# Three buffers for the halves of x, an earlier split of R, and the tile sets of each block built in one go, in a four-block modulated residual convolution

## The reference

```python
for k in range(4):                       # blocks L0 .. L3, each with its own weights
    out = x
    for i, typ in enumerate(('same', 'upsample', 'same', 'downsample')):
        out = _layer(out, cond_512, weights[i], biases[i], mod_w[i], mod_b[i], typ)
    x = x + out

def _layer(x, style, w, b, mw, mb, typ):
    s = style @ mw.T + mb                                  # a scale per sample and input channel
    weight = SCALE * w * s[:, None, :, None]
    demod = lax.rsqrt(jnp.sum(weight * weight, axis=(2, 3)) + EPS)
    weight = weight * demod[:, :, None, None]              # one 64 x 64 x 3 filter per sample
    if typ == 'same':         out = conv(x, weight, pad 1) + b
    elif typ == 'upsample':   out = blur(conv_transpose(x, weight, stride 2) + b, 2 * blur_k, (1, 1))
    elif typ == 'downsample': out = conv(blur(x, blur_k, (2, 2)), weight, stride 2) + b
```

## Time and profile before

| What | Value |
|---|---|
| median of 3 runs | 1443.01 us |
| the profiled execution's own time | 1441.61 us |
| its span, first to last instruction | 1439.8 us |
| busy: PE, PEld | 1405.6 us (98%), 1184.3 us (82%) |
| busy: DVE, ACT, POOL | 1017.6 us (71%), 701.8 us (49%), 380.8 us (26%) |
| granted TensorE clock | 1.00 (the 2.4 GHz level) in every slice |
| DMA queues, together | 39.65 MB, 28 GB/s |

### The profile page before, as it was taken

One profiled execution on the slowest core, in us unless ns is written; L12 is line 12 of the kernel. 1 busy time (PEld: TensorE's weight loads), 2 busy tenths in 40 slices (PEclk: granted clock), 3 DMA queues, 4 the chain that ended last, 5 costly groups with the idle time before them and its releaser, 6 DMA issues.

```text
span 1439.8 us, 21306 instructions
## 1 busy us (share of the span) xinstructions
PE 1405.6 (98%) x7436; PEld 1184.3 (82%) x7436; DVE 1017.6 (71%) x1634; ACT 701.8 (49%) x1132; POOL 380.8 (26%) x778
## 2 busy tenths in 40 slices
PE   5999999989999999999999999999999999999998
PEld 4777878878888888888888888888888888888886
DVE  8887978876676676677576676676676676676674
ACT  5445444536545445445555445445555444444454
POOL 4533332252322121221321222121231311212121
PEclk9999999999999999999999999999999999999999
DMA  6000000001530000000241000000042000000004
GB/s 225 7 1 1 7 1 2 5 1 65 140 95 1 1 1 1 0 1 1 64 114 59 1 1 0 1 1 1 1 110 67 0 1 1 1 1 1 1 16 102
DMA packets 20632, 39.65 MB, mean 28 GB/s; under 512 B 1840, under 2 KB 3248, under 8 KB 20528
## 3 DMA queue, kind: packets, MB, share of 16 engines
q1 hardware_dynamic: 20096, 37.87, 9.2%
q10 hardware_dynamic: 432, 0.43, 0.1%
HBM read 21.48 MB, written 16.81 MB: 27 GB/s over the span
## 4 chain that ended last, share of the span: by engine, by line
PE 90%; DVE 6%; ACT 1%; issue 1%; DMA 0%; POOL 0%; ACTq 0%; POOLq 0%; DVEq 0%
PE ps L361 28%; PE ps L363 27%; PE ps L362 27%; PE ps L368 3%; PE ps L367 3%; PE ps L458 1%; PE ps L477 1%; DVE gl L811 1%; DVE xl L763 1%; PE ps L468 1%; DVE vl L795 1%; DVE vh L794 1%; DVE gl L815 0%; PE ps L448 0%; ACT vh L595 0%
## 5 line engine op out<-in xcount | busy, mean ns | idle before, releaser
L575 ACT ACTIVATE zh<-ps,t_bx 128x512 fp32r<-128x512 f32 x256 | 176.3, 689 | 680.6 <-PE ps L363 676.8
L361 PE MATMUL ps<-zh,gh 128*128 128x512 f32 x1024 | 411.5, 402 | 0.2 <-DVE gl L815 0.2
L363 PE MATMUL ps<-zh,gl 128*128 128x512 f32 x1024 | 404.4, 395 | 0.0
L362 PE MATMUL ps<-zl,gh 128*128 128x512 f32 x1024 | 404.3, 395 | 0.0
L769 DVE SCALAR_TENSOR_TENSOR zl<-ps,t_bx,zh 128x512 fp32r<-128x512 f32 x256 | 190.6, 745 | 93.3 <-ACT zh L575 91.7
L363 PEld LDWEIGHTS ps<-zh,gl 128*128 128x128 f32 x1024 | 194.2, 190 | 46.1
L362 PEld LDWEIGHTS ps<-zl,gh 128*128 128x128 f32 x1024 | 193.9, 189 | 41.3
L779 DVE SCALAR_TENSOR_TENSOR X<-ps,t_D,X 128x511 f32<-128x511 f32 x256 | 190.7, 745 | 51.6 <-PE ps L363 51.4
L361 PEld LDWEIGHTS ps<-zh,gh 128*128 128x128 f32 x1024 | 193.0, 189 | 41.4 <-issue 0.3
L361 PE MATMUL ps<-xh,w0h 128*128 128x512 f32 x512 | 206.6, 403 | 8.1 <-DVE xl L763 8.1
L363 PE MATMUL ps<-xh,w0l 128*128 128x512 f32 x512 | 203.3, 397 | 0.0
(11 more groups left out here) (143 smaller groups left out, 2017.7 us busy)
## 6 DMA issues: line engine op xcount, KB each, us to landing
X<-x_in SPq DMA_DIRECT2D x32, 513.0 KB, 6.4
out_x<-X SPq DMA_DIRECT2D x64, 256.5 KB, 4.0
pk<-taps_in SPq DMA_DIRECT2D x3, 512.0 KB, 11.9
pk<-pack_in SPq DMA_DIRECT2D x3, 352.0 KB, 11.1
pk<-sets_in SPq DMA_DIRECT2D x4, 192.0 KB, 2.4
pk<-taps_in SPq DMA_DIRECT2D x2, 144.0 KB, 4.6
pk<-pack_in ACTq DMA_DIRECT2D x1, 224.0 KB, 3.1
w3f<-w_in SPq DMA_DIRECT2D x1, 192.0 KB, 10.5
```

Of the source, the lines that this page charges most:

```text
L361: pe.matmul(out_ap, ah, bh, start=first, stop=False, skip_group_check=True)
L362: pe.matmul(out_ap, ah, bl, start=False, stop=False, skip_group_check=True)
L363: return pe.matmul(out_ap, al, bh, start=False, stop=last, skip_group_check=True)
L575: act.activation(zh[n % 2][:, ZPAD:ZPAD + M], ps[:, ZP + n % 2, :], IDENT, bias=tab["bx"][:, k, b:b + 1]).then_inc(s["zhi"], 1)
```

## The change

Three parts. (1) `xh` and `xl` have three buffers each, and `xhi` and `xlo` run for sample n+3 in turn n, where it was n+2; `xhi(n+3)` waits for `conv0(n)`, as `xhi(n+2)` did before. Ahead of the loops ACT and DVE each make sample 2 as well: ACT between `w3hi(1)` and `ghi(0)`, DVE between the setup stage BIAS_S and `vfull(1)`. (2) SPLIT_R moves from slot 11 to slot 9, behind BIAS_U. (3) Each set of three taps is built in one turn: set 0 in turn 12 (from 12 and 15), set 1 in turn 16 (from 15, 16 and 19). For block 0 tap 2 of set 0 moves from turn 1 to turn 0, which leaves POOL's order as it was. SP loads the small set of blocks 1 to 3 in slot 2 in place of 4. PE's instruction order is the same.

```diff
-BUILD = {12: ((0, 0), (0, 1)), 15: ((0, 2), (1, 0)), 16: ((1, 1),), 19: ((1, 2),)}
-BUILD_FIRST = {0: ((0, 0), (0, 1)), 1: ((0, 2),), 2: ((1, 0), (1, 1)), 3: ((1, 2),)}
+BUILD = {12: ((0, 0), (0, 1), (0, 2)), 16: ((1, 0), (1, 1), (1, 2))}
+BUILD_FIRST = {0: ((0, 0), (0, 1), (0, 2)), 2: ((1, 0), (1, 1)), 3: ((1, 2),)}
...
-               8: (SPLIT_W,), 9: (BIAS_U,), 10: (BIAS_S,), 11: (SPLIT_R,)}
+               8: (SPLIT_W,), 9: (BIAS_U, SPLIT_R), 10: (BIAS_S,)}
...
-        xh = [sb(f"xh{i}", [128, XW + 1], F32R) for i in range(2)]
-        xl = [sb(f"xl{i}", [128, XW + 1], F32R) for i in range(2)]
+        xh = [sb(f"xh{i}", [128, XW + 1], F32R) for i in range(3)]
+        xl = [sb(f"xl{i}", [128, XW + 1], F32R) for i in range(3)]
...
-            return n // PS if n >= 0 and n % PS == 4 and n // PS < NBLK else None
+            return n // PS if n >= 0 and n % PS == (4 if n < PS else 2) and n // PS < NBLK else None
...
-                if n >= 2:
-                    act.wait_ge(s["conv0"], n - 1)
-                act.activation(xh[n % 2][:, 0:XW], X[:, sl, :], ACT.Copy, scale=tab["S0"][:, k, b:b + 1]) \
+                if n >= 3:
+                    act.wait_ge(s["conv0"], n - 2)
+                act.activation(xh[n % 3][:, 0:XW], X[:, sl, :], ACT.Copy, scale=tab["S0"][:, k, b:b + 1]) \
...
             w3hi(1)
+            xhi(2)
             ghi(0)
...
-                if n + 2 < NN:
-                    xhi(n + 2)
+                if n + 3 < NN:
+                    xhi(n + 3)
...
             setup(0, BIAS_S)
+            xlo(2)
             vfull(1)
...
-                if n + 2 < NN:
-                    xlo(n + 2)
+                if n + 3 < NN:
+                    xlo(n + 3)
```

More of the change, by code:

```diff
@@ L379, in conv0 @@
                     m = products(ps[:, ZP + b, :], w0h[:, k, w, :], w0l[:, k, w, :],
-                                 xh[b][:, d:d + M], xl[b][:, d:d + M], d == 0, d == 1)
+                                 xh[n % 3][:, d:d + M], xl[n % 3][:, d:d + M], d == 0, d == 1)
                 m.then_inc(s["conv0"], 1)
@@ L762, in xlo @@
                 dve.wait_ge(s["xhi"], n + 1)
-                dve.scalar_tensor_tensor(xl[n % 2][:, 0:XW], X[:, sl, :], tab["S0"][:, k, b:b + 1],
-                                         xh[n % 2][:, 0:XW].bitcast(F32), ALU.mult, ALU.subtract).then_inc(s["xlo"], 1)
+                dve.scalar_tensor_tensor(xl[n % 3][:, 0:XW], X[:, sl, :], tab["S0"][:, k, b:b + 1],
+                                         xh[n % 3][:, 0:XW].bitcast(F32), ALU.mult, ALU.subtract).then_inc(s["xlo"], 1)
             def zlo(n):
```

## The result

The changed kernel takes 1421.41 us (median of 5 runs, 1421.18 to 1422.54); the kernel before, timed beside it, 1443.01 (5 runs, 1441.73 to 1444.75). The ratio is 0.9852, 95% interval 0.9838 to 0.9867. One run of the kernel before in a later series took 2492.08 us at a mean granted clock of 0.57 and is left out of every comparison. The profiled executions differ by 20.2 us (own time 1441.61 against 1421.41; span 1439.8 against 1419.6).

A forecast was written before the change was run, and what follows sets the result against it. PE, busy 1405.6 of 1439.8 us, was taken as the bound. Split -5.5, buffers with builds -5.5 and -1.4, start +0.6 summed to -11.8 us: 1431.2 us from the median 1443.01, range 1429.0 to 1434.5.

The forecast's parts named there:

- the split: SPLIT_R in slot 9, in DVE's idle time before `vf`: three PE waits for `rdl` go, -5.5 us.
- what happens to the waits for `xl` and `zl`: Three buffers, counted with the builds moved: all ten `xl` waits end, no `zl` wait replaces them, -6.9 us.
- Rival B: Turns 15 to 17: PE waits for `zl` of sample 15, three times 1.4 us; 1435.4 us, chance 0.08.
- the start and the ends: Start: earlier `xl` lengthens the `vl` wait, +0.6 us; gathered ends ready at 141.8 to 142.8, before PE wants them.
- the step on the builds: Turns 12 and 16: one-turn sets free DVE's turn 14, 2.6 us; second set ends at 138.9, cost 0.
- rivals A and D: A: second set makes `ze` late, 1433.8 us, chance 0.14. D: late ends starve PE at line 448, slower, 0.02.
- what STYLE's COPY lost: Turn 16, beside the second build set: COPY slowed by 0.5 us; 1.3 us possible by the port lock rule.
- the change can move only the 34.2 us in which PE is idle: Whole kernel: PE's order and instructions stay, so its 1405.6 us of busy time was taken as fixed.
- That is the most that can be had behind the start: From 40 us on: PE's waits for `xl`, `rdl` and `ze`, 13.6 us in all, cap the gain, about 0.9%.

The follow-up runs named there:

- buffers_only: Changed kernel with build tables, `sets_at` and setup slots of before, so only the three buffers and earlier samples; 1437.97 us, ratio 0.9966.
- buffers_split: Changed kernel with the build tables and `sets_at` of the kernel before, keeping the buffers and SPLIT_R in slot 9; 1427.46 us, ratio 0.9894.
- layout_only: Kernel before with three tiles allocated for each half of x but two used, no instruction changed; 1436.57 us, ratio 0.9956.
- after_old_layout: Changed kernel with its third buffers allocated behind all other tiles, which lie as in the kernel before; 1427.76 us, ratio 0.9893.
- pad_vg_4096: Kernel before with an unused tile of 4096 bytes a partition ahead of `w3q`; 1442.28 us, ratio 1.0001.
- pad_vg_64: Kernel before with an unused tile of 64 bytes a partition ahead of `w3q`; 1438.26 us, ratio 0.9978.
- tap1_pad32: `after_tap1_slot5` with an unused tile of 32 bytes ahead of `w3q`; 1417.23 us, ratio 0.9827 to the kernel before.
- after_tap1_slot5: Changed kernel with `xlo(2)` behind `vlo(1)` and R_TAP1 moved from setup slot 3 to 5; 1419.1 us, ratio 0.9844 to the kernel before.
- after_xlo2_late: Changed kernel with `xlo(2)` moved behind `vlo(1)` in the start; 1420.9 us, ratio 0.9855 to the kernel before.

## Why the prediction was wrong, step by step

**Right: the split.** No wait for `rdl` is left, SPLIT_R lies in the hole before `vf` of turn 9 (1.46 us to spare; 0.9 were reckoned), and the part alone gives 6.2 us where the step said 5.5.

**Right: what happens to the waits for `xl` and `zl`.** All ten end, and PE does not fall on `zl`, as the builds no longer touch DVE's turn 14. Rival B named its own condition, that DVE's lateness was not POOL's doing; `buffers_only` and `buffers_split` show both sides of it, three waits for `zl` of 1.56 us with the old builds, none with the new. But the step booked the gain under the buffers, though it said that 4.9 us hang on the third part, and most of it belongs to the builds alone: they alone give 7.3 us by the medians (4.3 to 9.2 by the interval) and 7.0 by the starts of matmuls, and the third buffer what is left, four waits of 0.5 us.

**Right: the start and the ends.** The wait for `vl` is 2.70 (forecast 2.7). The wait for `ze` is 1.60, forecast 1.3: the end of the wait at 53.07 brings PE there 0.82 us sooner, not the 0.54 of its bracket. The second set ends at 136.70 and the gather at 140.59, and PE's line 448 stands at 142.91: the set is covered, as the step on the builds said; rivals A and D did not happen.

**Right by luck: what STYLE's COPY lost.** The prediction took 0.5 us from the longest COPY of the earlier trace rows. In turn 16 the COPY starts at 133.75, beside a build instruction that ends at 134.04, and itself ends at 134.09. In block 2 the two end at 223.50 and 223.56, and the COPY at 40.53 in the kernel before ends 0.05 us behind a build instruction too. So what it loses is not a slowdown of a certain size but the rest of the GpSimd instruction in whose time it falls, and in turn 16 little was left of that. The slowed `xl` show the same: each of the ten in the kernel before ends 0.55 to 0.56 us behind the end of a POOL instruction, as these two of the kernel before, POOL and then DVE (they end at 120.21 and 120.76):

```profile
119.16 1.05 POOL L999 TENSOR_TENSOR pk<-pk,misc 128x512 f32<-128x512 f32 x1
```

```profile
119.33 1.43 DVE L763 SCALAR_TENSOR_TENSOR xl<-X,t_S,xh 128x513 fp32r<-128x513 f32 x1
```

The Trainium skill ("SBUF — State Buffer", section "Who interferes with whom") has the port pair locked for the whole GpSimd instruction, with the other side fully blocked; the trace agrees, as these ends show. A COPY that came at the start of a build instruction could by these rows have lost up to 1.3 us; none here did.

**Wrong: "the change can move only the 34.2 us in which PE is idle", and of the 13.6 us of waits, "That is the most that can be had behind the start".** PE's busy time fell by 9.1 us. The step put at nothing two terms of the sum, without a reason.

First, the size of a wait. The prediction took its brackets for what a wait costs. A bracket counts from the modelled end of the matmul before, 0.40 us after its start, while the next would have started 0.23 after it. Before, 118.81 was the start of the last matmul and 120.82 that of the next: 2.01 us, bracket 1.62. After, it is 118.88 and 119.12: 0.24. The wait cost 1.77. That is 0.17 us for each of 13 waits, 2.2 us. The matmul behind it follows at 0.34 (120.82 to 121.16) in place of 0.23 (119.12 to 119.35), 0.1 us each time; with the three short stops that have no bracket this makes 1.8 in all. The two matmuls of the kernel before:

```profile
118.81 0.40 PE L363 MATMUL ps<-zh,gl 128*128 128x512 f32 x1
...
121.16 0.40 PE L362 MATMUL ps<-xl,w0h 128*128 128x512 f32 x1
```

Second, and larger, the place of the tiles. The sentence took the distance between matmuls as given. The third buffers move w3, V and G from a multiple of 128 bytes to 64 behind one, by the addresses in the compiled programs. `layout_only` shows this alone to be worth 6.4 us, `after_old_layout` its absence 6.3, and the pair of pads that it is the place, not the number of tiles: 64 bytes matter, 4096 don't. Mean distance between starts of matmuls from 412 to 1390 us (own working from the traces):

| Kernel | w3, V, G at, bytes mod 128 | matmuls with `vh`, ns | `conv0(72)` to `conv0(250)`, us |
|---|---|---|---|
| before | 0 | 119.8 | 965.3 |
| pad_vg_4096 | 0 | 119.8 | 964.9 |
| after_old_layout | 0 | 119.8 | 963.4 |
| layout_only | 64 | 117.6 | 960.2 |
| pad_vg_64 | 64 | 117.5 | 961.1 |
| after | 64 | 117.6 | 959.0 |
| tap1_pad32 | 96 | 116.0 | 958.2 |

The first two rows and `layout_only` and `pad_vg_64` still hold two waits of 0.5 us in that stretch, 1.5 us in all. In `layout_only` 1540 recorded matmuls of 256 columns at 2.3 ns make 3.5 of the 5.1 us; the other 1.6 lie in the matmuls of 512 columns, whose tiles moved as well. `pad_vg_64`, in which `xh`, `xl` and `zh` stayed, is 0.9 us behind `layout_only` there.

**Not foreseen: the clock.** In the profiled execution of the changed kernel, PE's granted clock is at the lower of its two levels (1.2 in place of 2.4 GHz) for 3.4 us behind the wait for `ze`. In 6 us it is 0.72 on average:

```profile
60.00:66.00 6.00, 6.00 (x22) 0.72 0.11 33
```

Nine matmuls from 60.79 to 64.43 take 3.64 us; at 0.235 each they would take 2.1. So this drop (0.28 of 6 us, 1.68) costs 1.5 us, as much as the wait of 1.60 ahead of it. The profiled execution of the kernel before has none, with waits of up to 2.07 us. But this is not a price of the change. `pad_vg_64` has the instructions and waits of the kernel before, and in its profiled execution the clock falls behind the wait of 1.96 us for `rdl` at 292.03, which in `pad_vg_4096` and `layout_only` (1.96 both) and in the kernel before (1.97) it does not. PE of `pad_vg_64` in that stretch, with a granted clock of 0.83:

```profile
290.00:300.00 10.00, 8.04 (x41) 0.83 0.01 2
```

And of the 41 runs of the kernel before in the four series, 17 had the full clock throughout and took 1440.83 to 1441.82 us; the other 24, with a mean clock of 0.997 to 0.999, took 1441.65 to 1444.26. The profiled execution that the prediction read had the full clock too, and its 1441.61 us lies within the range of the 17.

By the profiled executions, 11.8 forecast, 6.6 for the place, 2.2 and 1.8 for the size of the waits, less 1.5 for the clock, 0.3 for `ze` and 0.4 at the start, make 20.2 us, as measured. The medians differ by 1.4 more, 21.6: the median of the kernel before lies 1.4 above its profiled execution, and the changed kernel was profiled at its median. That the 1.4 are drops of the clock fits the 41 runs; the five runs themselves have no clock on record.

**What stays open.** Why the place of an operand sets the pace of a matmul isn't settled: whether it is the address of V and G itself or its relation to that of the weights (at 32 in all kernels that were looked at) was not tried, nor were more than three places; and as one long shift alone was tried, by 4096 bytes, it may be the address modulo another divisor of 4096 than 128. And what decides whether a wait is followed by the lower clock isn't either: the wait of 2.1 us for `vl` is followed by it in `after_tap1_slot5` and not in `after_xlo2_late`, in one profiled execution of each.

## What to carry to other kernels

A new buffer is two changes: allocate it without using it, and take that kernel for the "before"; then try a spare tile of 32 or 64 bytes, which adds no instruction. Reckon a wait of a pipelined engine by the starts of the instructions on both sides, less their usual distance, and not by its bracket. Where a wait ends with several late things behind it, ask first which engine made them late: here moving POOL's work out of DVE's turn freed more than a third buffer did. And look at the clock of every run before a microsecond is explained: a profiled execution without a drop is no fair "before" for one with it.

## What was not expected of the hardware

- A matmul of 256 columns on fp32r halves follows the one before at 119.8, 117.6 or 116.0 ns by the place of its tiles, at 0, 64 or 96 bytes mod 128, at full granted clock. With no instruction changed, `pad_vg_64` is 3.2 us faster and `layout_only` 6.4.
- A single drop of the granted clock costs 1.5 us here. It comes after waits of 1.6 to 2.7 us, in some executions and not in others: behind the same wait for `rdl` in `pad_vg_64` and not in the kernel before.
- GpSimd's work on SBUF stretches VectorE's (`gl` 0.36 to 1.37 us, `xl` 0.75 to 1.44) by a wait for the end of the GpSimd instruction: the slowed COPYs end 0.05 us behind it, the slowed `xl` 0.55. How much one loses depends on where in that instruction it falls.
